# Attention stage of a four-stage block: decay terms read as broadcast running maxima from DRAM instead of built on TensorE, and four heads' scores per step

## What is computed

```python
log_f = log_sigmoid(fg)                       # per head and token
log_f_cum = concat([0, cumsum(log_f, axis=2)], axis=2)
fg_mat = log_f_cum - transpose(log_f_cum)
log_D = where(ltr, fg_mat[:, :, 1:, 1:], -inf) + transpose(ig)
max_log_D = max(log_D, axis=-1, keepdims=True)
D = exp(log_D - max_log_D)
C = (qh @ kh.T) / sqrt(dh) * D
normalizer = maximum(abs(C.sum(-1, keepdims=True)), exp(-max_log_D))
h = (C / (normalizer + EPS)) @ vh             # then a norm over each head
```

## Time and profile before

| | |
|---|---|
| median of three runs | 2001.84 us |
| span of the profiled execution | 2011.2 us (it has no other time of its own; 9.4 us over the median) |
| PE busy | 1902.8 us (95%) |
| DVE busy | 1397.5 us (69%) |
| ACT busy | 803.5 us (40%) |
| POOL busy | 641.2 us (32%) |
| attention stage | about the first 751 us of the span |

### The profile page before, as it was taken

The page is one execution under the profiler, slowest core; times in us unless marked ns, Lnnn a source line. Parts: engine busy times, 40 slices in busy tenths (PEclk is TensorE's granted clock), DMA queues, the critical chain, the costliest instruction groups (busy, mean ns, idle before and its releaser), DMA issues. The chain is left out here.

```text
span 2011.2 us, 35222 instructions
## 1 busy us (share of the span) xinstructions
PE 1902.8 (95%) x13798; PEld 1623.6 (81%) x13798; DVE 1397.5 (69%) x2837; ACT 803.5 (40%) x1504; POOL 641.2 (32%) x507
## 2 busy tenths in 40 slices
PE   5799999999999999999999999799999989988997
PEld 3578888888888888999999998577777787767997
DVE  7687888888888865655455555588877857774664
ACT  5555555555555442312222222355444543232332
POOL 2433344333333331000000001477656720003563
PEclk6699999999999999999999999899999978999999
DMA  4212121111212115222322223544444444324675
GB/s 155 88 43 84 65 75 64 64 64 64 64 64 84 65 43 168 95 95 95 105 95 103 87 96 111 198 129 148 149 134 132 160 160 136 115 81 161 161 194 71
DMA packets 111750, 214.64 MB, mean 107 GB/s; under 512 B 14242, under 2 KB 34786, under 8 KB 110562
## 3 DMA queue, kind: packets, MB, share of 16 engines
q1 hardware_dynamic: 104194, 195.30, 28.9%
q0 software_dynamic: 7392, 17.11, 4.2%
HBM read 136.11 MB, written 76.34 MB: 106 GB/s over the span
## 5 line engine op out<-in xcount | busy, mean ns | idle before, releaser
L1257 PE MATMUL psum<-kv,toep 128*128 128x288 f32 x1280 | 324.0, 416 | 22.3 <-ACT yx L1570 13.7
L1257 PEld LDWEIGHTS psum<-kv,toep 128*128 128x128 f32 x1280 | 247.8, 195 | 95.8 <-ACT yx L1570 16.0
L184 PE MATMUL psum<-xn_t_h,w_gate_h 128*128 128x256 f32 x768 | 232.9, 303 | 1.3 <-DVE xn_th L315 1.3
L184 PE MATMUL psum<-xn_t_h,w_up_h 128*128 128x256 f32 x768 | 217.6, 283 | 0.0
L185 PE MATMUL psum<-xn_t_l,w_up_h 128*128 128x256 f32 x768 | 217.5, 283 | 0.0
L186 PE MATMUL psum<-xn_t_h,w_gate_l 128*128 128x256 f32 x768 | 217.5, 283 | 0.0
L185 PE MATMUL psum<-xn_t_l,w_gate_h 128*128 128x256 f32 x768 | 217.4, 283 | 0.0
L186 PE MATMUL psum<-xn_t_h,w_up_l 128*128 128x256 f32 x768 | 216.7, 282 | 0.0
L177 POOL TENSOR_TENSOR rstd<-rstd,minus_half 128x2 f32<-128x2 f32 x48 | 35.2, 733 | 513.6 <-DVE rstd L173 513.6
L298 ACT ACTIVATE xn_th<-psum 128x256 f32<-128x256 f32 x192 | 73.6, 383 | 310.2 <-PE psum L186 309.1
L1105 POOL TENSOR_SCALAR_AFFINE_SELECT operands<-operands 128x512 f32<-128x512 f32 x128 | 93.9, 733 | 323.0 <-ACT operands L848 323.0
(11 more groups left out here) (313 smaller groups left out, 4750.9 us busy)
## 6 DMA issues: line engine op xcount, KB each, us to landing
toep<-ssm_padded_scratch SPq DMA_DIRECT2D x64, 256.0 KB, 3.6
kx<-in_ctx_pairs SPq DMA_DIRECT2D x32, 384.0 KB, 4.9
x_scratch<-x_all SPq DMA_DIRECT2D x21, 512.0 KB, 2.8
x_all<-in_x SPq DMA_DIRECT2D x16, 512.0 KB, 3.8
operands<-in_ctx_t SPq DMA_DIRECT2D x16, 512.0 KB, 4.9
xn_t_scratch<-xn_t_h SPq DMA_DIRECT2D x16, 512.0 KB, 2.7
xn_t_scratch<-xn_t_l SPq DMA_DIRECT2D x16, 512.0 KB, 3.6
xn_t_h<-xn_t_scratch SPq DMA_DIRECT2D x16, 512.0 KB, 3.7
```

Of the source, the lines that this page charges most:

```text
L184: pe.run.matmul(out, lhs[0], rhs[0], start=first, stop=False)
L1257: ins = pe.run.matmul(out, w[:, (o - k) * P:(o - k + 1) * P], pairs, start=(k == 0), stop=(k == o))
```

## The change

The decay products on PE, the "parts" and "rows" stages, `mg`, `pick`, `row_of` and their setup go. Instead:

- DVE writes M to a tile of its own, `mx`. SP stores it to DRAM (`store_max`, 16 KB), and loads for each four heads their rows of it onto all 128 partitions (`load_max`, 512 KB), into three tiles `mb`, two of which lie on the place of `xn_t2` that is unused until the second half.
- "norms" on PE also turns g to token partitions; ACT copies it to `gt`.
- "exp" is now per four heads: eight ACT exponentials, four of 128x256 and four of 128x128, out of `mb` with scale -1 and with g of the key as a per-partition bias. The POOL mask and the DVE product are per four heads too (128x1024 and 128x1536).
- "score" makes the scores of four heads at once in banks 0 to 3. "step" is gone.
- Queries are loaded by `load_q` into `xq` and normalised there; x itself is loaded a second time, later, for the residual.
- The written order changes throughout. The bank choice of gate_up changes from tiles 0 and 2 in bank 6 to tiles 1 and 5.

```diff
@@ slots(b): before
-    yield [("step", a, 0), ("exp", a, 0), ("turn_h", e, 3), ("sums", e), ("gate_up", f, 0), ("turn_shares", f),
-           ("load_x", o), ("load_ctx", o)]
-    yield [("step", a, 1), ("exp", a, 1), ("share", f, 0), ("gate_low", f, 0), ("spread", e, 0),
-           ("gate_up", f, 1), ("share", f, 1)]
-    yield [("step", a, 2), ("exp", a, 2), ("normalise_x", o), ("spread", e, 1), ("load_values", o),
-           ("gate_low", f, 1), ("gate_up", f, 2), ("share", f, 2)]
-    yield [("step", a, 3), ("exp", a, 3), ("weighted", a, 0), ("apply_x", o), ("gate_low", f, 2), ("gate_up", f, 3),
-           ("share", f, 3), ("residual", e)]
...
-    yield [("step", a, 7), ("turn_x", e, 0), ("weighted", a, 2), ("turn_x", e, 1), ("gates_log", o), ("exp", a, 7),
-           ("decays", o), ("down", f, 0), ("router", e), ("parts", o), ("values", o)]
-    yield [("step", a, 8), ("logits", e), ("down", f, 1), ("store_x2", f), ("turn_h", a, 2), ("rows", o),
-           ("norms", o), ("shares", e)]
-    yield [("weighted", a, 3)]
@@ slots(b): after
+    yield [("score", a, 0), ("turn_h", e, 3), ("sums", e), ("gate_up", f, 0), ("turn_shares", f),
+           ("load_max", a, 3), ("normalise_x", o), ("load_x", o), ("load_ctx", o)]
+    yield [("weighted", a, 0), ("share", f, 0), ("gate_low", f, 0), ("spread", e, 0), ("apply_x", o),
+           ("gate_up", f, 1), ("share", f, 1), ("exp", a, 2)]
+    yield [("turn_h", a, 0), ("score", a, 1), ("turn_query", o, 0), ("spread", e, 1), ("load_values", o),
+           ("gate_low", f, 1), ("turn_query", o, 1), ("gate_up", f, 2), ("share", f, 2)]
+    yield [("weighted", a, 1), ("gates", o), ("load_q", o + 1), ("gate_low", f, 2), ("gate_up", f, 3),
+           ("share", f, 3), ("exp", a, 3), ("residual", e)]
+    yield [("turn_h", a, 1), ("score", a, 2), ("gates_log", o), ("gate_low", f, 3), ("gate_up", f, 4),
+           ("share", f, 4), ("decays", o), ("store_max", o), ("statistics", e)]
...
+    yield [("weighted", a, 2), ("gate_low", f, 4), ("norms", o), ("gate_up", f, 5), ("share", f, 5),
+           ("normalise", e), ("load_max", o, 0), ("load_max", o, 1), ("load_max", o, 2)]
+    yield [("turn_h", a, 2), ("score", a, 3), ("gate_low", f, 5), ("turn_x", e, 0), ("sum_values", o),
+           ("exp", o, 0)]
+    yield [("down", f, 0), ("turn_x", e, 1), ("weighted", a, 3), ("router", e), ("values", o)]
+    yield [("logits", e), ("down", f, 1), ("store_x2", f), ("exp", o, 1), ("shares", e)]
@@ banks
-    banks.plan((name, b, at[0]), ((6, 5), (5, 4), (5, 5))[b][at[0]] if b < 3 else 6)
+    banks.plan((name, b, at[0]), (5, 7)[at[0]] if b < 3 else 6)
...
-    banks.plan((name, b, 0, at[0]), 5 + (at[0] % 2 if b >= B - 2 else at[0] in (0, 2)))
+    banks.plan((name, b, 0, at[0]), 5 + (at[0] % 2 if b >= B - 2 else at[0] in (1, 5)))
@@ tensor_attention
-            for t in range(ST):
-                ins = pe.run.transpose(bank_t[bank][:, t * NH:(t + 1) * NH], nm[:, t * P:(t + 1) * P],
-                                       ident[0:NH, 0:NH])
+            for i, rows_ in enumerate((nm, gm)):
+                for t in range(ST):
+                    j = i * ST + t
+                    ins = pe.run.transpose(bank_t[bank][:, j * NH:(j + 1) * NH], rows_[:, t * P:(t + 1) * P],
+                                           ident[0:NH, 0:NH])
...
+        elif name == "score":
+            g = at[0]
+            pe.wait_ge(scored, b * QUADS + g)
             for piece in range(2):
+                for j in range(4):
+                    r = head_rows(j)
+                    ins = pe.run.matmul(blocks(bank_t[j], piece), c_t[b % 2][r, g, piece * P:(piece + 1) * P],
+                                        q_t[b % 2][r, g, piece * P:S], start=True, stop=True,
+                                        tile_position=(r.start, 0))
+            ins.then_inc(score_made, 1)
@@ scalar_attention
-            act.run.activation(e_t[n % 4][:, :, :], psum[:, 0:2 * BANK].rearrange(
-                "p (j c) -> p j c", j=2)[:, :, 0:3 * P], ACT.Exp).then_inc(decay_exp, 1)
+        elif name == "exp":
+            g = at[0]
+            n = b * QUADS + g
+            bank, filled, emptied, m = banks.at("norms", b)
+            act.wait_ge(emptied, m + 1)
+            act.wait_ge(max_loaded[n % 3], 16 * (n // 3 + 1))
+            quad_filled(act, n - 2)
+            for j in range(4):
+                for t in range(ST):
+                    out = blocks(e_q[n % 2][:, j, :], t)
+                    top_ = mb[n % 3][:, j, t * P:S]
+                    if t == 0:
+                        top_ = top_.rearrange("p (a c) -> p a c", a=ST)
+                    ins = act.run.activation(out, top_, ACT.Exp, bias=gt[b % 2][:, t, 4 * g + j:4 * g + j + 1],
+                                             scale=-1.0)
+            ins.then_inc(decay_exp, 1)
@@ vector_attention
-            c = e_t[n % 4][:, :, :]
-            dve.run.scalar_tensor_tensor(c, psum[:, 2 * BANK:4 * BANK].rearrange("p (j c) -> p j c", j=2)[
+            c = e_q[n % 2][:, :, :]
+            dve.run.scalar_tensor_tensor(c, psum[:, 0:4 * BANK].rearrange("p (j c) -> p j c", j=4)[
                 :, :, 0:3 * P], float(DH) ** -0.5, c, ALU.mult, ALU.mult).then_inc(scored, 1)
@@ sync_attention
+    def store_max(b):
+        sp.wait_ge(norm_log, b + 1)
+        sp.run.dma_start(mx_d[b], mx[:, :]).then_inc(max_stored, 16)
+
+    def load_max(b, g):
+        n = b * QUADS + g
+        sp.wait_ge(max_stored, 16 * (b + 1))
+        if n >= 3:
+            sp.wait_ge(decay_exp, n - 2)
+        row = mx_d[b]
+        sp.run.dma_start(mb[n % 3][:, :, :], bass.AP(row.tensor, row.offset + 4 * g * S,
+                                                     [[0, P], [S, 4], [1, S]])).then_inc(max_loaded[n % 3], 16)
```

More of the change, by code:

```diff
@@ L507, in build_program @@
                 shares_ready = signal("shares_ready")
[L514 to L520, removed]
@@ L521, in build_program @@
-                first_slots = [
[L522 to L527, removed]
-                    [("step", 0, 5), ("exp", 0, 5), ("weighted", 0, 1), ("normalise_x", 2), ("weights_high", 3)],
-                    [("step", 0, 6), ("exp", 0, 6), ("turn_h", 0, 1), ("apply_x", 2), ("weights_low", 3), ("load_weights", 5)],
-                    [("step", 0, 7), ("exp", 0, 7), ("weighted", 0, 2), ("weights_high", 4)],
-                    [("step", 0, 8), ("turn_h", 0, 2), ("weights_low", 4), ("load_ctx", 2)],
-                    [("step", 1, 0), ("exp", 1, 0), ("weighted", 0, 3), ("turn_query", 2, 0)],
-                    [("turn_h", 0, 3), ("step", 1, 1), ("exp", 1, 1), ("sums", 0), ("turn_query", 2, 1)],
-                    [("step", 1, 2), ("exp", 1, 2), ("spread", 0, 0), ("gate_keys", 2), ("weights_high", 5), ("weights_low", 5)],
-                    [("step", 1, 3), ("exp", 1, 3), ("weighted", 1, 0), ("spread", 0, 1), ("load_values", 2), ("gates", 2)],
-                    [("step", 1, 4), ("exp", 1, 4), ("turn_h", 1, 0), ("residual", 0), ("gates_log", 2)],
-                    [("step", 1, 5), ("exp", 1, 5), ("weighted", 1, 1), ("statistics", 0), ("decays", 2)],
-                    [("step", 1, 6), ("exp", 1, 6), ("normalise", 0), ("turn_h", 1, 1), ("sum_values", 2), ("parts", 2)],
-                    [("step", 1, 7), ("exp", 1, 7), ("turn_x", 0, 0), ("turn_x", 0, 1), ("weighted", 1, 2), ("rows", 2),
-                     ("norms", 2), ("values", 2)],
-                    [("step", 1, 8), ("router", 0), ("turn_h", 1, 2), ("logits", 0), ("gate_up", 0, 0), ("shares", 0)],
-                    [("weighted", 1, 3)]]
@@ L818, in scalar_attention @@
                         elif name in ("apply_x", "normalise"):
-                            first, out, turn, ready = ((0, xq, "turn_query", xq_ready) if name == "apply_x" else
-                                                       (ST, xn2, "turn_x", xn_ready))
+                            first, src, out, turn, ready = ((0, xq, xq, "turn_query", xq_ready) if name == "apply_x" else
+                                                            (ST, x_t[b % 4], xn2, "turn_x", xn_ready))
                             act.wait_ge(ln_inverse, norm_no["normalise_x" if name == "apply_x" else "statistics", b])
@@ L981, in vector_attention @@
                             if b:
[L982 to L984 removed]
+                                bank, filled, emptied, n = banks.at("norms", b - 1)
+                                dve.wait_ge(filled, n + 1)
+                                dve.wait_ge(max_stored, 16 * b)
                             dve.settle(dve.run.scalar_tensor_tensor(la[:, :], fg[:, :], 0.0, la[:, :], ALU.min, ALU.subtract))
```

247 lines of the change are left out of this document (101 added, 146 removed).

## The result

The changed kernel takes 2171.4 us (median of four runs, 2168.4 to 2176.3) where the kernel before took 2002.8 in the same comparison: a ratio of 1.084, 95% interval 1.083 to 1.086. It is slower by 8.4%, and all of the loss lies in the attention stage.

What follows compares the result with a forecast made beforehand. PE bound the steady attention batches, DVE next. Period 46.5 becomes 41.7 plus 15.9 of waits, 57.6, plus 3.4 of clock: 14.5 more, thirteen times +189, -1, -5; span 2194, median 2185 us, range 2045 to 2260.

Steps and rivals of the forecast that it cites:

- PE's own work: PE per period: 8.0 us of old stages go, 3.4 of score and 0.2 of norms come; 41.7 us without waits.
- row groups don't run together: Rival, score stage on PE: 1.7 us instead of 0.85, +3.4 per batch, at most +50 us; no chance of its own.
- Exponential of four heads: Eight ACT instructions: 2.7 us plus at most 0.23 each for bias from a tile; half gives 3.6, taken as 3.0.
- (a): PE at norms, right behind weighted 2, waits for decays through ACT's and DVE's queues: 7.65 us per period, least 4.3.
- (b): PE at turn_query 1 waits for ACT's copy out of bank 6: 2.7 us, 4.9 with tanh 1 late behind apply_x.
- (c): PE at weighted 0 waits for DVE's shares and product after the last down tile: 1.05 us.
- (d): PE waits at turn_x 0 for late statistics 0.8, router 0.85, logits 0.65: together 2.3 us.
- Clock: PE's new waits bring two short stretches of half clock, 3.4 us per period; bounds nothing to 10 us.
- half clock spreads: Rival: half clock costs PE 10 us more per period, as in 60 to 110 us before; 2270 us, chance 0.12.
- Start: Before the steady batches: pairs' round trips and parts go, store, load and eight ACT instructions come; -5 us (-15 to +10).
- savings realised: Rival: queues have unseen slack, PE keeps its 4.4 us, new waits under 4.8 per period; 1927 us, chance 0.09.
- waits at their least: Rival: ACT and DVE free of backlog, full clock, period 51.3 us; 2058 us, chance 0.2.

Runs made afterwards that it cites:

- reordered: Changed kernel, same operations in a new written order in the steady batches, second query transpose in bank 7: 2049.1 us, 1.022 of the kernel before.
- sixteen exponentials: Changed kernel with each exponential cut in two, sixteen ACT instructions per four heads instead of eight, same elements: 2214.1 us.
- bank experiment: Changed kernel with the second turn_query of a steady batch in bank 7, not in bank 6 behind the first: 2111.5 us.
- quarter loads: Changed kernel, from the fourth load of maxima on only one of four heads' rows loaded, 128 KB in place of 512 KB: 2168.2 us.
- norms later: Changed kernel with the stage norms moved behind score 3, before turn_x 0, in the steady batches: 2155.0 us.
- second reordering: The changed kernel's operations in a further new order: gate_up tiles alternating banks 5 and 6, exp 1 behind weighted 0, turn_x and score 3 ahead of turn_h 2: 2045.5 us.
- both cuts: First reordered kernel with one head's exponentials written to all four in three instructions, and DVE's product made for two of four heads: 2027.2 us.

## Why the prediction was right

The verdict and the mechanism held, and the sum came near: 2185 forecast, 2171.4 measured. The mechanism is shown by the edits to order and banks alone, which take back 122 of 169 us, and by the waits, which stand where the walk had them. How close the number came is in part luck, as the last lines of this list show. Step by step, per period where nothing else is said:

- **PE's own work**: forecast 41.7 us; 42.5 in the changed kernel and 43.0 (49.33 less idle of 6.3) in the reordered one. The score stage took 0.88 us (784.07 to 784.95; forecast 0.85), which also ends the rival "row groups don't run together". The net saving against the 46.3 us of before was mis-sized by about 1 us, 3.3 to 3.8 instead of 4.4. A likely part is that a matmul's own 0.28 us isn't covered by the next at each of eight waits, where flowing ones start 0.12 apart, 0.16 each; this was not tried by itself.
- **Exponential of four heads**: 2.87 us, forecast 3.0. The form with its bias from a tile takes 114 ns more than L298's (497 against 383), which is half of the bound, as taken; L298 also reads PSUM and is no exponential, so the bias's own share isn't shown. The Trainium skill's page quoted there ("ScalarE: Activation LUTs", "What ACT_TABLE_LOAD costs") gave an estimate of 2.8; the trace's 2.87 agrees.
- **DVE product**: 1.754 us, forecast 1.75.
- **(a) norms and weighted 2**: 4.65 + 1.47 = 6.1, forecast 7.65. The chain was as walked: ACT's part took 7.6 us (783.4 to 791.03) for 8.2, DVE's with the hops 4.2 (to 795.19) for 4.75, decays 2.7 of it for 3.1; PE's own part took 5.7 for 5.3. The experiment with sixteen exponentials confirms that ACT stands last in the chain, with DVE's own queue 1.20 us behind it. One reading was wrong: in the order before, both down tiles stand between decays and norms, not one of 4 us, so the change took away more cover than the prediction says. The sum doesn't use that.
- **(b) turn_query**: 1.85 + 1.94 = 3.8, forecast 4.9, split over two waits: the first is for the bank that DVE's gate_up tile leaves, which the walk had put into the delay of ACT. The second was shown by the bank experiment.
- **(c), (d)**: 0.88 against 1.05; turn_x, router and logits together 1.7 (20.4 us over twelve periods) against 2.3.
- **Sum of waits**: 12.5, forecast 15.9. Mis-sized by 3.4, each of the terms a little high.
- **Clock**: 4.0, forecast 3.4, and in exactly the form taken: two short stretches per period. The Trainium skill's page "TensorE: Matmul & The Clock Gate", section "HAM oscillation", tells of a loop whose wait puts every round back to the slow clock; the trace agrees, with two such stretches in each of the twelve periods. The bank experiment shows that the clock doubled the price of one wait; the rival "half clock spreads" didn't come.
- **Loads**: 5.1 us each, forecast 3.8, by the nearest row; hidden all the same.
- **Thirteen periods**: +12.47 each is +162, forecast +189.
- **Start**: first store less one period, 167.83 - 58.98 = 108.9, before 147.38 - 46.51 = 100.9: +8 where -5 was taken, inside its bounds. What makes up the 8 us stays open: the changed kernel has 103.9 with quarter loads, but 104.3 with norms later and 108.6 with the second query bank, both with full loads, so kernels whose code is the same for their first 110 us differ by as much as the quarter loads do.
- **Batches 13 to 15**: 982.00 - 875.57 = 106.4 against 815.57 - 705.45 = 110.1: -3.7, forecast -1.
- **The tail, "0, their code is the same"**: 1184.7 against 1195.6 us. This step failed, by -11; the last section has it.

162 + 8 - 3.7 - 10.9 = +155.5, which is 2166.7 - 2011.2. The forecast of the span, 2194, was 27 too high: the thirteen periods alone make 27 of it, and the start (13 too low) is cancelled by the tail (11 too high) and batches 13 to 15 (3 too high), which is luck. Luck too is that the new span lay under its median, not over it as before; that gave half of the 27 back.

The rival on the other side, savings realised, needed new waits of under 4.8 us per period. Even the reordered kernels have 6.3 and, with clock, 4.2 + 1.7 of them. The rival "waits at their least", 2058 us, is about what the reordered kernels reach; in the written order neither ACT nor DVE was free of its backlog.

## What to carry to other kernels

With one written order for all engines, a consumer set right behind a late producer can cost more than the arithmetic that a change saves, as here: walk each new dependence through every queue that stands between, and put full-clock work (here a down tile) into the gap. Removing one wait pays only if nothing else is owed by the same late queue; and a wait of 2 us on TensorE can cost 4. Before moving work to an engine because it is busy only 40% of the time, ask whether its bursts now stand ahead of something that the bound engine needs.

## What the runs showed of the hardware

**The tail's length follows its half-clock time.** Its work is the same in all kernels, yet it takes 1182 to 1196 us. From the last batch's store to the end, the kernel before, then the one with the second query bank:

```profile
815.57:2011.20 1195.63, 1130.83 (x6570) 979.73 (x6570) 755.82 (x1347) 393.92 (x746) 357.18 (x244) 0.97 0.41 127
```

```profile
926.76:2109.80 1183.04, 1123.04 (x6570) 973.77 (x6570) 755.35 (x1347) 394.13 (x746) 355.53 (x244) 0.98 0.41 128
```

Half clock in these stretches, by the clock record, and their length: 52.7 us, 1181.9 (sixteen exponentials); 54.2, 1183.0 (second query bank); 59.0, 1184.7 (after); 67.9, 1188.5 (reordered); 78.4, 1193.2 (second reordering); 79.3, 1195.6 (before). Over all thirteen kernels a straight line gives 0.39 us of length for each us of half clock, and no kernel lies further off it than the quarter loads, 4.0 us below (74.8 and 1186.9). So code that a change doesn't touch varies here by up to 14 us between these executions, one of each kernel. What makes its clock fall more often in one than in another stays open.

**Short waits can bring the clock down too.** In the reordered kernel with both cuts, no listed wait in the twelve periods has over 1.0 us, and yet 41 us of half clock stand in them, at down 0, behind waits of 0.6 and 1.0; in the plain reordered kernel waits of 0.3 and 1.0 stand in the same places with the clock full, and so does one of 1.5 elsewhere in each period (L295 on `sel`). The timeline of PE in the former; a matmul of 128x512 takes 0.40 us at full clock (in the plain reordered kernel's down 0):

```profile
660.49 0.63 PE L184 MATMUL psum<-w_down_h,a_t_h 128*128 128x512 f32 x1
```

The length of one wait does not decide it, and these runs don't show what does.
